# Four graph layers on one core: edge loops unrolled to sixteen groups a round, block numbers decoded in pieces on TensorE, one weighted one-hot made on ScalarE

## The reference

```
layer 0: fwd = mlp(x[dst], x[src], e16);  bwd = mlp(x[src], x[dst], e16)       # 80 -> 64 -> 32, relu
         out = mlp(concat(segment_sum(fwd, dst), segment_sum(bwd, src)))       # 64 -> 64 -> 32
layer 1: tpw = mlp(e8)                                                         # 8 -> 64 -> 64 -> 256, silu
         out = x @ self weights + segment_sum(tensor product(x[src], e4, tpw), dst) / 4
layer 2: ten steps of h = 0.9 * norm * A (norm * h) + 0.1 * x,  norm = in-degree ** -0.5
layer 3: three steps of X = segment_sum(w[:, None] * X[dst], src)
```

## Time and profile before

| | |
|---|---|
| median of 3 runs | 4498.11 us (4493.66 to 4520.53) |
| profiled execution | 4511.84 us, its span 4510.1 us |
| busy share of the span | PE 69%, PEld 44%, DVE 56%, ACT 34%, POOL 45% |
| layer-0 loop (first to last L925) | 960.3 to 2437.8 us |
| layer-1 loop (first to last L1595) | 2525.1 to 3537.5 us |

### The profile page before, as it was taken

How to read it: one execution, slowest core, us unless ns; L and a number is a source line. 1 busy time by engine, 2 the same in 40 slices (tenths; PEclk the granted TensorE clock), 3 DMA queues, 4 the chain that set the end, 5 groups by cost and what they waited for, 6 DMA issues and landing times. The chain is left out here.

```text
span 4510.1 us, 106688 instructions
## 1 busy us (share of the span) xinstructions
PE 3111.8 (69%) x28819; PEld 1977.5 (44%) x28820; DVE 2512.7 (56%) x7841; ACT 1512.7 (34%) x3455; POOL 2049.9 (45%) x3286
## 2 busy tenths in 40 slices
PE   2420000257777777777777799999999449988998
PEld 1100000046666666666665355555555325542222
DVE  7842212466666666666665698989998514440000
ACT  0011111124333333333333577777777301100000
POOL 1047777534444444444442588888888400000000
PEclk9999999879888888888887798988998779998999
DMA  9101111134444443334341110110101450008673
GB/s 375 58 14 23 22 23 22 20 107 136 136 135 135 135 135 121 127 120 129 120 136 70 28 27 26 26 27 26 28 26 26 85 106 0 0 0 367 287 303 136
DMA packets 190491, 431.03 MB, mean 96 GB/s; under 512 B 32352, under 2 KB 143066, under 8 KB 177274
## 3 DMA queue, kind: packets, MB, share of 16 engines
q1 hardware_dynamic: 156988, 365.02, 23.1%
q0 software_dynamic: 32816, 61.65, 6.1%
q10 hardware_dynamic: 520, 2.80, 0.2%
HBM read 227.36 MB, written 136.86 MB: 81 GB/s over the span
## 5 line engine op out<-in xcount | busy, mean ns | idle before, releaser
L208 POOL DMA_INDIRECT sorted_edges<-s_record,s_index x400 | 476.1, 1190 | 370.6 <-issue 362.1
L809 POOL TENSOR_TENSOR e_part<-e_rest,e_part 128x256 bf16<-128x256 f32 x202 | 133.2, 659 | 785.6 <-ACT e_part L851 785.6
L1016 DVE TENSOR_TENSOR e_strip<-e_p_aw,e_strip 128x256 f32 x804 | 334.9, 417 | 269.3 <-issue 199.7
L1347 POOL TENSOR_SCALAR m_oh<-m_iotab,m_rec 128x128 bf16<-128x128 bf16 x812 | 474.5, 600 | 0.1
L2068 PE MATMUL r_p_o<-r_W,r_X 128*32 128x512 f32 (+1 forms) x1050 | 408.3, 549 | 41.4 <-DMA r_W<-dense_strips 39.2
L803 POOL TENSOR_TENSOR e_ohw<-e_oh,e_rec 128x512 bf16<-128x512 bf16 x408 | 420.7, 1059 | 10.5 <-DVE e_oh L993 7.8
L1793 PE MATMUL q_p_s<-q_A,q_g 128*96 128x512 bf16 (+1 forms) x1750 | 349.5, 357 | 102.8 <-DMA q_A<-dense_strips 101.5
L259 PE MATMUL s_p_t<-s_ident,s_oh_src 125*128 125x125 f16 x100 | 21.2, 284 | 504.3 <-issue 259.0
L1000 DVE TENSOR_SCALAR e_ohw<-e_p_iota,e_rec 128x128 bf16<-128x128 f32 x816 | 327.7, 403 | 0.0
L842 ACT ACTIVATE e_hid<-e_p_hid,e_b 128x512 f32<-128x512 f32 x204 | 140.3, 688 | 557.8 <-PE e_p_hid L901 557.8
L1793 PEld LDWEIGHTS q_p_s<-q_A,q_g 128*96 128x96 bf16 x1750 | 197.7, 123 | 235.0 <-issue 105.8
(11 more groups left out here) (309 smaller groups left out, 7423.0 us busy)
## 6 DMA issues: line engine op xcount, KB each, us to landing
r_W<-dense_strips SPq DMA_DIRECT2D x18, 6400.0 KB, 17.7
e_strip<-e_zeros SPq DMA_DIRECT2D x26, 3200.0 KB, 13.8
dense_strips<-e_strip SPq DMA_DIRECT2D x25, 3200.0 KB
sorted_edges<-s_neg SPq DMA_DIRECT2D x1, 40560.0 KB, 161.8
e_rec<-sorted_edges POOLq DMA_DIRECT2D x208, 130.0 KB, 2.4
m_rec<-sorted_edges SPq DMA_DIRECT2D x208, 130.0 KB, 2.1
q_A<-dense_strips POOLq DMA_DIRECT2D x25, 800.0 KB, 46.2
sorted_edges<-s_record,s_index POOLq DMA_INDIRECT x400
```

Source lines behind the costliest of these rows:

```text
L208: pool.indirect_dma_start(dram["edges"], bass.IndirectOffsetOnAxis(ap=index[s][:, c:c + 1], axis=0), record[s][:, c, :], None).then_inc(s_ ...
L1016: i = V.tensor_tensor(at, p_aw[u][:, v, :].rearrange("p (k c) -> p k c", k=2), at, ALU.add)
L1347: i = g.tensor_scalar(oh[s][:, t, :], iotab[:, :], rec[s][:, t, CDST:CDST + 1], None, ALU.is_equal)
```

## The change

It has three parts.

1. U becomes 16: a round is sixteen groups. The depth of the record and one-hot buffers and of the loads stays eight, as SLOTS = U // 2. There are sixteen `loaded` semaphores, one for each group of a round, made once for both loops; a wait for a load of group s is `n + (U - 1)` where it was `n * 2 + 14`. Layer 1's loads are issued as layer 0's were: eight ahead of the loop, and in the loop those of group j + 8.
2. On PE in layer 0 the block numbers of a group are decoded in three pieces: the load and the source block behind `second`, two targets behind `dense`, the other two at the start of the next step behind `turn`. DVE's decoding stays.
3. In layer 0 `weigh_hi` moves from DVE, where it compared and multiplied the iota row, to ACT, where it scales the one-hot that DVE has made by the weight, four tiles in a row at the end of the step for group j+5.

```diff
-U = 4 * TB // G
+U = 8 * TB // G
+SLOTS = U // 2
-BODIES = (TILES + NB * (TB - 1)) // TB + U
+BODIES = (TILES + NB * (TB - 1)) // TB + SLOTS
 def round_end(last):
-    return ((last + 3) >> 2) * U + 1
+    return ((last + 7) >> 3) * U + 1
+def packed_blocks(nc, engine, table, n, s):
+    return engine.value_load(table[0:1, bass.ds(body_of(nc, n, s), 1), TPACK[s % 2]], min_val=0, max_val=(1 << (G + 1) * BITS) - 1)
+def unpacked_block(nc, engine, packed, t):
+    value = (packed >> (BITS * t)) & ((1 << BITS) - 1) if t < G else packed >> (G * BITS)
+    return nc.snap(value, engines=[engine.engine], min_val=0, max_val=NB - 1)
...
-        rec = in_turn(lambda s: sb(f"rec{s}", [P, G, REC], F32), U)
-        oh = in_turn(lambda s: sb(f"oh{s}", [P, G, 2, P], BF16), U)
+        rec = in_turn(lambda s: sb(f"rec{s}", [P, G, REC], F32), SLOTS)
+        oh = in_turn(lambda s: sb(f"oh{s}", [P, G, 2, P], BF16), SLOTS)
-        loaded = [sem(f"loaded{s}") for s in slots]
+        loaded = dram["e_loaded"]
...
             def load(n, s):
-                onehots.before(pool, n, s, U)
-                weighted_hi.before(pool, n, s, U)
...
+                onehots.before(pool, n, s, SLOTS)
+                weighted_hi.before(pool, n, s, SLOTS)
...
-                    load(*group(n, j + U))
+                    load(*group(n, j + SLOTS))
...
+            def weigh_hi(n, s):                                   # on ACT
+                onehots.after(act, n, s)
+                aw_done[1].before(act, n, s, 4)
+                act.sem_inc(prime, 1)
+                for t in range(G):
+                    i = nc.scalar.activation(ohw[s][:, t, 0, :], oh[s][:, t, 0, :], ACT.Copy, scale=rec[s][:, t, CW:CW + 1])
+                weighted_hi.set_by(i)
-                staged(n, j, (middle, 2), (relu1, 4), (copies, 5), (relu2, 3))
+                staged(n, j, (middle, 2), (relu1, 4), (copies, 5), (relu2, 3), (weigh_hi, 5))
...
             def work(n, j, blocks):                               # on PE
                 staged(n, j, (turn, 5))
+                if blocks:
+                    src, packed, dsts = blocks
+                    dsts = dsts + [unpacked_block(nc, pe, packed, t) for t in range(len(dsts), G)]
                 if j + 4 >= 0:
-                    hidden(*group(n, j + 4), blocks)
-                later = blocks_of(nc, pe, table, *group(n, j + 5)) if j + 5 >= 0 and j + 1 < U else None
-                staged(n, j, (second, 3), (sums, 1), (dense, 2))
-                return later
+                    hidden(*group(n, j + 4), (src, dsts))
+                staged(n, j, (second, 3))
+                more = j + 5 >= 0 and j + 1 < U
+                if more:
+                    packed = packed_blocks(nc, pe, table, *group(n, j + 5))
+                    src = unpacked_block(nc, pe, packed, G)
+                staged(n, j, (sums, 1), (dense, 2))
+                return (src, packed, [unpacked_block(nc, pe, packed, t) for t in range(2)]) if more else None
+            def blocks_now(n, s):
+                packed = packed_blocks(nc, pe, table, n, s)
+                return unpacked_block(nc, pe, packed, G), packed, []
-                    blocks = work(n, j, blocks if j else blocks_of(nc, pe, table, *group(n, 4)))
+                    blocks = work(n, j, blocks if j else blocks_now(*group(n, 4)))
...
-            def weigh_hi(n, s, t):                                # on DVE
-                if t == 0:
-                    aw_done[1].before(dve, n, s, 4)
-                    dve.sem_inc(prime, 1)
-                i = V.tensor_scalar(ohw[s][:, t, 0, :], p_iota[:, 0:P], rec[s][:, t, CSRC:CSRC + 1], rec[s][:, t, CW:CW + 1],
-                                    ALU.is_equal, ALU.mult)
-                if t == G - 1:
-                    weighted_hi.set_by(i)
...
-                    if j + 4 >= 0:
-                        weigh_hi(*group(n, j + 4), t)
...
-            with sp.Fori(1, round_end(last) + U, U) as n:         # layer 1
-                for s in slots:
-                    onehots.before(sp, n, s, U)
...
+            for s in range(SLOTS):
+                load(1, s)
+            with sp.Fori(1, round_end(last), U) as n:
+                for j in slots:
+                    load(*group(n, j + SLOTS))
```

More of the change, by code:

```diff
@@ L751, in _ @@
             sp.wait_ge(d_start, 32)
-            last = sp.value_load(starts[0:1, NB:NB + 1], min_val=NB, max_val=BODIES - U)
+            last = sp.value_load(starts[0:1, NB:NB + 1], min_val=NB, max_val=BODIES - SLOTS)
             def one_strip(k):
@@ L829, in _ @@
             act.wait_ge(d_start, 32)
-            last = act.value_load(starts[0:1, NB:NB + 1], min_val=NB, max_val=BODIES - U)
+            last = act.value_load(starts[0:1, NB:NB + 1], min_val=NB, max_val=BODIES - SLOTS)
             act.wait_ge(d_b, 288)
@@ L866, in _ @@
             pe.wait_ge(d_start, 32)
-            last = pe.value_load(starts[0:1, NB:NB + 1], min_val=NB, max_val=BODIES - U)
+            last = pe.value_load(starts[0:1, NB:NB + 1], min_val=NB, max_val=BODIES - SLOTS)
             pe.wait_ge(d_b, 288)
@@ L1568, in _ @@
             dve.wait_ge(d_start, 32)
-            last = dve.value_load(starts[0:1, NB:NB + 1], min_val=NB, max_val=BODIES - U)
+            last = dve.value_load(starts[0:1, NB:NB + 1], min_val=NB, max_val=BODIES - SLOTS)
             MM = MUL * MUL
@@ L2141, in build @@
         dram["sent"] = [ctx.enter_context(nc.semaphore(f"sent{k}")) for k in range(2)]
+        dram["e_loaded"] = [ctx.enter_context(nc.semaphore(f"e_loaded{s}")) for s in range(U)]
         dram["a_loaded"] = ctx.enter_context(nc.semaphore("a_loaded"))
```

52 lines of the change are left out of this document (27 added, 25 removed).

## The result

The kernel after takes **4431 us** (median of 4 runs, 4419 to 4444); the kernel before, run beside it, 4496 us (4487 to 4521). The ratio is 0.985, 95% interval 0.980 to 0.990: faster by about 1.5%. The profiled execution took 4443.8 us (span 4442.1), before 4511.8 (4510.1), so the two profiles can be compared: 68 us less span.

The account below looks back on a forecast made before the run. It took TensorE's queue, held by the decode, and round boundaries to bound layer 0, VectorE layer 1. Terms -20 - 109 - 12 + 66 = -75 off the 4498.11 us median gave 4423, stated as 4425; range 4340 to 4535.

Parts of the forecast that it names:

- The rounds of layer 0, -20: Layer-0 loop: 13 rounds of 16 groups in place of 25 of 8 take 1443 us instead of 1463, -20.
- The decode in pieces, -109: Layer-0 TensorE: splitting and moving the decode saves 0.6 us on 14 of 16 steps in 13 rounds, -109 us.
- The hold of 0.8: Layer-0 TensorE: its queue stands full behind L929's eight fp32 matmuls for 0.8 of the 6.44 us step.
- the idle of 1.43: Layer-0 TensorE: idle of 1.43 us in a quick step, just before L925, put down to late issue by the decode.
- TensorE's fetch in layer 0, costed at nothing: Layer-0 round boundary: the doubled body may be fetched each round, +46 us bare, but hidden by the 3.96 us wait for VectorE.
- The weighted one-hot, -12: Layer-0 boundary: moving it off VectorE saves 0.9 us a round, -12 us; ScalarE's operations, estimated at 0.3 us, stay hidden.
- Layer 1, +66: Layer-1 loop: +36 more groups, -49 fewer boundaries, +46 VectorE code fetch, +33 lower clock; +66 us, from -13 to +120.
- What it said the profile would show: Layer-0 L925 intervals near 5.7 us, its idle mostly gone, fetch packets at boundaries, layer-1 VectorE idle 3 to 5 us.
- The queue freed but not the period: Layer-0 rival: TensorE's own work at low clock bounds many steps, decode brings 0.2 us a step; 4496 us, chance 0.24.
- The larger gain: Rival: layer-0 decode brings 1.0 us a step (-182), layer-1 clock falls no more than now (+33); 4317 us, chance 0.12.
- Code fetching decides: Rival: both loops stall for code at branches, layer 1 +120, layer 0 +46, decode only 0.1 a step; 4626 us, chance 0.08.
- The decode does not really move: Layer-0 TensorE rival: the register work is merged again, so the decode gains nothing; 4532 us, chance 0.11.

Follow-up runs that it names:

- e1: The kernel after with the layer-1 edge loop back at 8 groups a round, layer 0 staying at 16; 4341 us, ratio 0.966.
- e3: The kernel before with only TensorE's decode in pieces; 8 groups a round, weighted one-hot on VectorE; 4380 us, ratio 0.977.
- e2: The kernel before with sixteen groups a round in both loops and nothing else; 4642 us, ratio 1.036.
- e6: The kernel after with 8 groups a round in both loops; decode in pieces and weighted one-hot on ScalarE stay; 4374 us, ratio 0.973.
- e5: The kernel after with the weighted one-hot back on VectorE; 16 groups and the decode in pieces stay; 4433 us, ratio 0.988.
- e4: The kernel before with only the weighted one-hot moved to ScalarE; 8 groups, decode as before; 4481 us, ratio 0.996.
- e7: The kernel before with TensorE's whole decode moved in one piece behind the second product, ahead of the sums; 4390 us, ratio 0.976.
- e10: e1 with TensorE decoding block numbers once a round in layer 0, so hidden-layer products use wrong blocks; 4196 us, ratio 0.931.
- e11: e6 with VectorE decoding the four target numbers only once a round, so sums go to wrong blocks; 4227 us, ratio 0.940.
- e9: e1 with TensorE's whole decode in one piece behind the sums instead of in pieces; 4628 us, ratio 1.025.

## Why the prediction was right, and which of its steps were not

The sum was -75 us and the range 4340 to 4535; the profiled span fell by 68, the median by 65. The mechanism of the forecast, TensorE's queue held by the decode against fetches of the longer bodies, is what e1 to e3 show. But the steps in it were off in both directions:

- **The rounds of layer 0, -20.** Alone they are +54 (e2); beside the pieces they are -31 (e6 to after). The 8 groups (+52) and the 12 boundaries (-67) were priced about right for the rounds alone; the inner steps, taken as unchanged, grew by 0.3 us. Beside the pieces they grow as much, but the boundaries are dearer at 8 groups, 9.3 us above two steps (20.5 less 2 x 5.6, with VectorE at their end) against 7.0 at 16 (18.6 less 2 x 5.8): 25 x 9.3 - 13 x 7.0 is 142 us and not 67.
- **The decode in pieces, -109.** At 8 groups that number is met (e3), by other parts: 6 inner steps x 25 x 0.81 = -121 (a mean of 6.41 to 5.60), and +13 at the boundary. In the kernel it was priced for, 16 groups, it is 1532 to 1338 = -194 (e2 to e5): the inner steps go from a mean of 6.80 to 5.96, 14 x 13 x 0.84 = -153, and the two intervals of the boundary from 21.7 to 18.7, -40. So 0.6 was too small, and the boundary was missing from the sum: the prediction let the decode hide behind VectorE there, and at 16 groups VectorE no longer ends it. The hold of 0.8 was the right guide to the step, for the idle of 1.43 turned by half into slow issue. That these two terms together come out (-129 predicted, 54 - 194 = -140 measured) is luck: each is off by some 80 us, in opposite directions.
- **TensorE's fetch in layer 0, costed at nothing because VectorE's wait hides it.** The queue packets came as said (14 a round). In the whole change the boundary did not grow (20.2 to 18.6); with the rounds alone it did (21.7). But its cover is gone: TensorE's wait for VectorE's adds is 0.4 us in all, and the branch of 4.9 us now ends the boundary.
- **The weighted one-hot, -12.** Between nothing and that: the boundary is unchanged in e4, 0.1 us shorter in e6 against e3, and the loop -2 (e3 to e6) or -3 (e5 to after). No run shows the 0.9 us a round. ScalarE's operation takes 0.40 us, the upper end and not the 0.3 I took, and is hidden all the same. By the Trainium skill's page "ScalarE: Activation LUTs", What ACT_TABLE_LOAD costs, an ACTIVATE takes 186 ns and 0.833 ns a column, and each operand that points at a value per partition adds 93 ns: for one such operand and 128 columns an estimate of 386 ns. The trace agrees, with 400.
- **Layer 1, +66.** +85 in the profile of after, +74 in e2, +53 in e5, about 100 between the medians at 8 and 16 groups. The terms of fetch and clock are the right ones, but their sizes were not. The interval behind the branch went from 5.55 to 7.8, 2.3 a round or 29 us, where 46 stood. The later ones lie 8.3 us a round above 4.48 in after and 5.9 in e5, where the 3.0 of before were to become 5.5: 69 and 38 us, where 33 stood. TensorE's own fetch (3.4 us at the branch, 4.32 of idle) stands beside VectorE's there; the prediction had VectorE's alone, and it is TensorE's standing still that comes before the low clock.
- **What it said the profile would show.** Intervals near 5.7, the idle ahead of the flow products gone, 0.3 us from the wait of the sums to that of the dense stage (1502.67 to 1502.95), 211 starts of L945, q8 packets at layer 0's boundary, q14 in layer 1, VectorE idle for 3.4 us there and the clock at 0.50 behind the stall: all there. Layer 1 grew by more than the 30 us set as the limit.
- **Rivals.** "The queue freed but not the period" (4496) is out by e3. "The larger gain" had the size of the decode (-182 for layer 0, measured -194) and was wrong on layer 1's clock. "Code fetching decides" is out as put, for the decode brings more than 0.1; but the longer rounds without the pieces are 3.5% slower (e2). "The decode does not really move" is out by e3 and e7; e10 shows that more than half of its cost, 0.9 of 1.5 us, is still there.

## What to carry to other kernels

In this kernel, register work on TensorE's sequencer is free only behind products that keep the engine busy long per instruction, and it comes back where the following products need a register operation each; a busy engine whose products come 0.12 us apart instead of 0.055 is waiting for its sequencer. Before a loop body is made longer, look at the instruction queues: a body that is resident at 8 groups and fetched at 16 can pay at each boundary more than the boundaries saved (layer 1 did, layer 0 beside the pieces did not), so choose the length for each loop by itself (here 16 and 8: 4341 us, 3.4% under the kernel before). And a body just over what stays resident is worth shortening: leaving out 92 of VectorE's 338 recorded instructions a round, which dropped part of the work, took 138 us off the loop, 90 of them the fetch; a form that keeps all the work was not tried. Last, look where periodic traffic falls: a flush that a boundary hid comes out in the middle of a longer round.

## What the runs showed of the hardware that was not expected

- VectorE's branch back is a record of 0.07 us whether its body is fetched again or not. The fetch is the gap behind it: the sequencer's next record comes 0.23 us later where the body stays (layer 1 before, both loops of e11) and 2.7 to 4.7 us later where it does not (medians of the runs). On TensorE the branch itself is longer: 0.22 us where the body stays, 3.4 to 3.5 in layer 1 at 16 groups and 4.1 to 6.4 in layer 0 (medians).
- Layer 1's body of TensorE is fetched at 1015 recorded instructions a round (279 of the sequencer and 736 matmuls; 1751 with the weight loads), layer 0's of 941 (e6; 1557 with them) is not. VectorE's is fetched at 338 and stays at 246 and 269. By the Trainium skill's page "Runtime: NRT & Kernel Launch", Instruction fetch mechanics, the windows hold 512 instructions in 32 KiB, and 2048 in 128 KiB for TensorE. The trace neither bears that out nor speaks against it. The bytes fetched each round are above those windows: 40 KB on VectorE (before, layer 0, five packets of 8 KB), and on TensorE after 143 KB in layer 1 and 223 KB in layer 0; TensorE's layer-0 body before came in once, in seven packets of 16 KB, 112 KB, and stayed. But what is fetched may be more than the body, and what is recorded less, so neither gives the length at which a body stops staying: the packets on q8 and q14 only tell whether it does.
- The register load of the packed word takes 0.29 us, but in layer 0 some take about 1: over 0.6 us are 41 of TensorE's 202 before, 44 of 210 after, 50 in e2, 70 in e11, none in layer 1. All 611 such loads of TensorE in the layer-0 loops of the fourteen kernels overlap packets of q1, SyncE's flush and clearing of a strip of 3.2 MB each; 167 others overlap them and stay under 0.6, and not one slow load lies outside. In layer 1 q1 carries only the records, at a DMA share of 0.10, and no load is slow. Code fetch is not the cause, for e11 fetches next to none, and neither is an overlap with VectorE's load from the same table: in e3, 122 of TensorE's loads overlap one and are quick. No run moved or dropped the flush, so that it is the cause is not shown. In the kernels of 8 groups most of these loads fall on the two intervals of the boundary (49 of 51 in e6); at 16 groups more than half fall in the middle, after in the ninth and eleventh intervals of a round (6.7 and 6.8 us, the other inner ones 5.6 to 6.2).
- The same decode of 1.7 us costs a step 0.7 us in one piece behind eight fp32 products (e7, 5.65 against 4.95 in e10), 1.5 ahead of them (before, 6.49) and 1.65 behind the 24 short ones that follow (e9, 6.6).
